# A perceiver block on one core: TensorE's batch loop turned to begin with its products, and the second correction group moved ahead of the seventh key-value part

## The chip, the core and the metric

The kernel runs on one NeuronCore of a Trainium2 chip. That core has TensorE (PE, matrix products), VectorE (DVE), ScalarE (ACT), GpSimd (POOL) and SyncE (SP, which here issues every DMA). Each engine takes its instructions in program order, and they meet only at semaphores. The metric is the device time of one execution in microseconds (us), as the median over runs.

## The reference, cut to what matters

Three residual parts follow each other: a linear cross-attention of 8 × 64 queries on a context of 8 × 1601 rows, a distance attention over the batch, and a mixture of eight experts with causal attention. The change lies in the first part and at its end.

```python
q = (decoder_seq @ Wq.T + bq)          # layer-normed x, 8 batches of 64 rows
k = (encoder_seq @ Wk.T + bk)          # ctx_1024, 8 batches of 1601 rows
v = (encoder_seq @ Wv.T + bv)
kv = jnp.einsum('bthd,bthe->bhde', k, v)            # 16 heads of 32 x 32 per batch
att = jnp.einsum('bqhd,bhde->bqhe', q, kv) * scale
x = x + layer_norm(att + decoder_seq, gamma, beta)
```

## The kernel before, in words

The kernel never forms k and v. For each batch b it makes the Gram matrix G = C^T C of the context (512 x 512), then M = G Wv^T, then the head blocks of Wk M, which are the 16 blocks of kv without bias. Biases come in at the end as "corrections", made from row sums. Every fp32 product of the Gram matrix and of M is split in a high and a low part, so three products stand for one (lines 319 to 321).

On TensorE, one batch is made of these pieces:

- `gram(b)`, lines 844 to 871: 130 products of high and low parts of 13 row groups, about 20 us.
- `products_of(b)`: `m_part(b, 0..3)`, each 12 products of 512 columns (lines 319 to 321), with `mirror(b+1)` (line 885, ten transposes) after the second and `g_transposes(b+1)` (line 892, six transposes) after the fourth.
- `kv_part(b)`, line 923: 64 small fp32 products of 32 columns. The profile has two weight loads and two matmuls for each, so 128 of both, 256 instructions in about 1.3 us. It waits for ACT's copy of the fourth part of M (`m_copy`, line 570).

The pieces of neighbouring batches are interleaved. Batches 0 and 1 are begun in straight code, then a hardware loop (`pe.Fori`, line 951) runs five times over kv_part(b-2), gram(b), products_of(b-1) for b = 2 to 6, and kv_part(5) and gram(7) follow in straight code. In the loop the semaphore counts that are waited for depend on b and are worked out by register instructions. ACT, DVE, POOL and SP have loops of their own and are not turned.

After gram(7) comes the end of the first part, in straight code, written in an order by hand: `row_sums`, m_part(6, 0..3) with `mirror(7)` and `sum_rows` between, `group_corrections(0)` (line 995 two matmuls, line 1001 32 matmuls: batches 0 and 1), `g_transposes(7)`, `kv_part(6)`, `attend(0)` (line 1023), `group_corrections(1)` (batches 2 and 3), m_part(7, 0), `attend(1)`, `group_corrections(2)` (batches 4 to 6), m_part(7, 1), `attend(2)` and so on. group_corrections(n) needs ACT's `right_part(b)` (line 625) for all batches up to the group's last (rb_done), and the kept kv of these batches (kv_done). ACT's `group_spread(1)` (line 643) then spreads the result for `attend(1)`. ACT's order there: three right_parts, m_copy(6, 3), `last_gh_high` (lines 631, 632, 634: the high part of the last Gram matrix), four right_parts, group_spread(1). DVE makes the low part (`last_gl_low`, lines 1516 to 1520, with the copy of kv_part(6) on line 1406 between), which m_part(7, 0) waits for (gl_done). SP loads a weight (`owT`, line 370) once two correction groups are done.

Of the kernel before, what the change touches and what calls it, by code (L numbers as in the profile page):

```python
# [34 lines left out]
def perceiver_block(nc, a, out):  # L35

    B, S, D = a["x"].shape
# [20 lines left out]
    with ExitStack() as ctx:  # L58
# [189 lines left out]
        def head_block(t, c, j):  # L248

            return t[D1 * j:D1 * j + D1, D1 * c:D1 * c + D1]  # L250
# [11 lines left out]
        def right_of(b):  # L262

            return raw[0:64, 4 + b, :] if b < B - 1 else psum_tmp[0:64, :]
# [3 lines left out]
        def group_bank(n):  # L268

            return bank[(1, 2, 4)[n]][:, 0:P * (groups[n][1] - groups[n][0])]  # L270
# [245 lines left out]
        def _(act):  # L516
# [50 lines left out]
            def m_copy(b, ms=range(KC)):  # L567
                for m in ms:
                    act.wait_ge(m_mm, b * 4 + m + 1)
                    act.activation(mb[:, m, :], bank[6 + m % 2][:, :], ACT.Copy).then_inc(m_done, 1)  # L570
# [52 lines left out]
            def right_part(b):  # L623
                act.wait_ge(right_near, 1)
                act.activation(right_of(b), right, ACT.Copy, scale=batch_of[:, b:b + 1]).then_inc(rb_done, 1)

            def last_gh_high():
                act.wait_ge(m_mm, (B - 1) * 4)
                act.wait_ge(gl_done, (B - 1) * 3)
                act.wait_ge(g_add, B * 5)  # L630
                act.activation(upper(ghf, 5 * P), upper(g32f, 5 * P), ACT.Copy).then_inc(gh_done, 1)
                act.activation(last_block(ghf), last_block(g32f), ACT.Copy).then_inc(gh_done, 1)
                act.wait_ge(gt_mm, B)
                act.activation(lower(ghf), mir[:, 0:2, :].rearrange("p m n -> p (m n)")[:, 0:6 * P].rearrange("p (m n) -> p m n", m=3),
                               ACT.Copy).then_inc(gh_done, 1)

            def group_spread(n):

                act.wait_ge(r2_mm, n + 1)
                src = group_bank(n).rearrange("p (m d) -> p m d", d=D1)  # L640
                dst = kv[:, groups[n][0]:groups[n][1], :].rearrange("p b (c j d) -> p (b c) j d", j=4, d=D1)
                for j in range(4):
                    act.activation(dst[:, :, j, :], src, ACT.Copy, scale=headmask[:, D1 * j:D1 * j + 1]).then_inc(r2_act, 1)

            for b in range(3):
                right_part(b)
            m_copy(B - 2, (3,))
            last_gh_high()
            for b in range(3, 7):
                right_part(b)  # L650
            group_spread(1)
            m_copy(B - 1, (0,))
            group_spread(2)
            right_part(B - 1)
# [106 lines left out]
        def _(pe):  # L761
# [112 lines left out]
            def mirror(b):  # L874

                pe.wait_ge(cr_act, b * 2 + 2)
                pe.wait_ge(cr_dve, b + 1)
                c2, c3 = cross[:, 0, :], cross[:, 1, :]
                blk = lambda row, n: row[:, n * P:(n + 1) * P]
                c01 = cross[:, 2, :]  # L880
                for m, row in enumerate(((blk(c01, 0), blk(c01, 2), blk(c2, 0)),
                                         (blk(c01, 3), blk(c2, 1), blk(c3, 1)),
                                         (blk(c2, 2), blk(c3, 2), blk(c01, 1), blk(c3, 3)))):
                    for n, src in enumerate(row):
                        mm = pe.transpose(mir[:, m, n * P:(n + 1) * P], src, ident[:, :])  # L885
                mm.then_inc(mir_mm, 1)

            def g_transposes(b):

                pe.wait_ge(g_add, b * 5 + 5)  # L890
                for n, (row, col) in enumerate(((3, 0), (0, 1), (0, 2), (1, 2), (1, 3), (2, 3))):
                    mm = pe.transpose(mir[:, n // 4, (n % 4) * P:(n % 4 + 1) * P], g32[:, row, col * P:(col + 1) * P], ident[:, :])
                mm.then_inc(gt_mm, 1)

            def m_part(b, m, first):

                if first and m == 0:
                    pe.wait_ge(w_lo, 2)
                    pe.wait_ge(q_done, KC)
                    pe.wait_ge(ld_wk, 16)  # L900
                if m == 0:
                    pe.wait_ge(gl_done, b * 3 + 3)
                if not first and m == 0:
                    pe.wait_ge(kv_done, b)
                if not (first and m < 2):
                    pe.wait_ge(m_done, b * 4 + m - 1)
                for k in range(KC):
                    rows = slice(m * P, (m + 1) * P)
                    mm = three(pe, bank[6 + m % 2][:, :], gh[:, k, rows], gl[:, k, rows], wvh[:, k, :], wvl[:, k, :],
                               k == 0, k == KC - 1)  # L910
                mm.then_inc(m_mm, 1)

            def kv_part(b):

                pe.wait_ge(m_done, b * 4 + 4)
                last = isinstance(b, int) and b == B - 1
                if last:
                    pe.wait_ge(rb_done, B)
                for c in range(KC):
                    for k in range(KC):  # L920
                        for j in range(4):
                            cols = slice(c * P + D1 * j, c * P + D1 * j + D1)
                            mm = pe.matmul(head_block(bank[6], c, j), wk[:, k, cols], mb[:, k, cols],  # L923
                                           start=(k == 0 and not (last and c)), stop=(k == KC - 1 and not last), skip_group_check=last)
                if last:
                    for c in range(KC):
                        for j in range(4):
                            cols = slice(c * P + D1 * j, c * P + D1 * j + D1)
                            mm = pe.matmul(head_block(bank[6], c, j), left[:, cols], right_of(b)[:, cols],
                                           start=False, stop=True, skip_group_check=True)  # L930
                mm.then_inc(kv_mm, 1)

            def products_of(b, first, halfway, between):

                m_part(b, 0, first)
                m_part(b, 1, first)
                halfway()
                m_part(b, 2, first)
                m_part(b, 3, first)
                between()  # L940
# [7 lines left out]
            first_queries((2, 3))  # L948
            gram(1, False)
            products_of(0, True, lambda: mirror(1), lambda: g_transposes(1))  # L950
            with pe.Fori(2, B - 1) as b:
                kv_part(b - 2)
                gram(b, False)
                products_of(b - 1, False, lambda: mirror(b), lambda: g_transposes(b))
            kv_part(B - 3)
            gram(B - 1, False)

            def row_sums():

# [26 lines left out]
            def group_corrections(n):  # L986

                first, end = groups[n]
                if n == 0:
                    pe.wait_ge(bk_near, 1)  # L990
                    pe.wait_ge(rk_near, 1)
                if n == 2:
                    pe.wait_ge(gl_done, 3 * B)
                pe.wait_ge(kv_done, end)
                pe.matmul(group_bank(n), ident[:, :], kv[:, first:end, 0:P], start=True, stop=False, skip_group_check=True)
                pe.wait_ge(rb_done, end)
                at = group_bank(n).rearrange("p (b m) -> p b m", m=P)
                for c in range(KC):
                    for j in range(4):
                        cols = slice(c * P + D1 * j, c * P + D1 * j + D1)  # L1000
                        mm = pe.matmul(at[D1 * j:D1 * j + D1, :, D1 * c:D1 * c + D1], left[:, cols], raw[0:64, 4 + first:4 + end, cols],
                                       start=False, stop=True, skip_group_check=True)
                mm.then_inc(r2_mm, 1)
# [31 lines left out]
            m_part(B - 2, 3, False)  # L1035
            group_corrections(0)
            g_transposes(B - 1)
            kv_part(B - 2)
            attend(0)
            group_corrections(1)  # L1040
            m_part(B - 1, 0, False)
            attend(1)
            group_corrections(2)
# [766 lines left out]
```

## Time and profile before

| | us |
|---|---|
| median of three runs (590.27, 591.0, 598.87) | 591.0 |
| the profiled execution | 589.4 |
| its span | 587.6 |
| TensorE busy | 572.4 (97%) |
| VectorE, ScalarE, GpSimd busy | 346.8, 205.4, 221.2 |

The span runs from the first to the last instruction; 1.8 us of the profiled execution lie around it. The granted TensorE clock is 0.997 of full speed over the whole span, so nothing below hangs on it. "Busy" of TensorE counts matmuls whose ends are modelled. Of the DMA queues, q1 carries the data that SP issues, and q8 and q14 are of the kind "instruction": q8 brings 16 KB at a time (28 packets, 0.46 MB), q14 8 KB.

### The profile page before, as it was taken

To read this page: it belongs to the slowest core of one execution; us is meant where nothing else is said; L and a number is where in the kernel's file an instruction comes from. 1 tells how busy PE (TensorE), PEld (TensorE's weight loads), DVE (VectorE), ACT (ScalarE), POOL (GpSimd) and SP (SyncE) were. 2 spreads that over 40 slices of the span, in tenths; PEclk is the share of its full clock that TensorE was granted. 3 is DMA by queue.
4 is the path that set the end of the run, shared out by engine and by line. 5 is a ranking of instruction groups with operands and counts; after the bars stand their busy time and mean duration, and the time that the engine had idled before them with its cause. 6 is when DMAs were issued, how large, how long until landed. Compare 5 with 4: busy or idle time off the path is not lost.

```text
span 587.6 us, 11551 instructions
## 1 busy us (share of the span) xinstructions
PE 572.4 (97%) x4910; PEld 490.0 (83%) x4910; DVE 346.8 (59%) x405; ACT 205.4 (35%) x294; POOL 221.2 (38%) x182
## 2 busy tenths in 40 slices
PE   6999999999999999899999999999999999999997
PEld 6989888898989889797678987977888887888886
DVE  4896771826546182652687357567777346875741
ACT  4534343505234350522652351423441122434320
POOL 2599963565627265560425000203334543000000
PEclk9999999999999999999999999999999999999999
DMA  8763423142213324004210401206722312898601
GB/s 308 278 239 126 153 86 140 71 152 71 76 76 104 119 71 152 1 1 161 52 72 3 154 3 71 74 1 160 207 72 78 137 72 71 172 260 209 149 0 71
DMA packets 25284, 65.76 MB, mean 112 GB/s; under 512 B 2424, under 2 KB 2424, under 8 KB 22304
## 3 DMA queue, kind: packets, MB, share of 16 engines
q1 hardware_dynamic: 25248, 65.23, 34.9%
q8 instruction: 28, 0.46, 0.4%
q14 instruction: 8, 0.07, 0.1%
HBM read 64.05 MB, written 1.18 MB: 111 GB/s over the span
## 4 chain that ended last, share of the span: by engine, by line
PE 82%; POOL 5%; DVE 4%; issue 1%; POOLq 0%; ACT 0%; DVEq 0%
PE ps L319 17%; PE ps L321 16%; PE ps L320 16%; PE ps L844 8%; POOL psum_tmp L457 4%; PE ps L867 3%; PE ps L871 3%; PE ps L859 2%; PE ps L923 2%; PE ps L854 2%; PE ps L853 2%; PE ps L858 2%; PE ps L1141 1%; PE ps L885 1%; PE ps L1125 1%
## 5 line engine op out<-in xcount | busy, mean ns | idle before, releaser
L457 POOL TENSOR_TENSOR psum_tmp<-psum_tmp,raw 128x512 f32<-128x512 f32 (+1 forms) x88 | 139.7, 1588 | 31.9 <-DVE lo L1364 23.4
L844 PE MATMUL ps<-hi 128*128 128x256 f32 (+3 forms) x416 | 129.5, 313 | 4.9 <-ACT hi L536 4.9
L844 PEld LDWEIGHTS ps<-hi 128*128 128x128 f32 (+1 forms) x416 | 78.7, 190 | 5.3 <-ACT hi L536 4.9
L1364 DVE TENSOR_TENSOR lo<-raw,hi 128x2048 fp32r<-128x2048 f32 (+1 forms) x29 | 61.7, 2158 | 24.4 <-ACT hi L528 24.4
L319 PE MATMUL ps<-hi,gh 128*128 128x512 f32 x192 | 75.7, 394 | 0.0
L321 PE MATMUL ps<-hi,gl 128*128 128x512 f32 x192 | 74.8, 390 | 0.0
L320 PE MATMUL ps<-lo,gh 128*128 128x512 f32 x192 | 74.8, 390 | 0.0
L509 POOL TENSOR_TENSOR sx<-sx,raw 128x512 f32<-128x512 f32 x32 | 41.0, 1288 | 82.4 <-DVE raw L1701 82.4
L731 ACT ACTIVATE hi<-raw 128x2048 fp32r<-128x2048 f32 x14 | 26.8, 1913 | 91.9 <-PE ps L321 91.9
L319 PE MATMUL ps<-wvh,gh 128*128 128x512 f32 x128 | 51.1, 399 | 0.0
L321 PE MATMUL ps<-wvh,gl 128*128 128x512 f32 x128 | 50.1, 391 | 0.0
L320 PE MATMUL ps<-wvl,gh 128*128 128x512 f32 x128 | 50.0, 390 | 0.0
L528 ACT ACTIVATE hi<-raw 128x2048 fp32r<-128x2048 f32 (+1 forms) x29 | 44.0, 1559 | 10.3 <-DMA raw<-in_ctx 10.3
L1707 DVE TENSOR_TENSOR lo<-raw,hi 128x2048 fp32r<-128x2048 f32 x15 | 34.3, 2289 | 19.7 <-ACT hi L731 19.7
L544 ACT ACTIVATE par<-ps 128x512 f32<-128x512 f32 x14 | 7.6, 595 | 101.6 <-PE ps L871 101.6
L319 PEld LDWEIGHTS ps<-hi,gh 128*128 128x128 f32 x192 | 36.0, 188 | 7.8 <-issue 0.2
L321 PEld LDWEIGHTS ps<-hi,gl 128*128 128x128 f32 x192 | 36.0, 188 | 7.5
L320 PEld LDWEIGHTS ps<-lo,gh 128*128 128x128 f32 x192 | 36.1, 188 | 7.3
L867 PE MATMUL ps<-lo,hi 128*128 128x512 f32 (+1 forms) x104 | 41.5, 399 | 0.0
L1370 DVE COPY par<-ps 128x512 f32<-128x512 f32 x8 | 5.5, 690 | 60.7 <-PE ps L871 60.7
L871 PE MATMUL ps<-lo,hi 128*128 128x512 f32 (+1 forms) x104 | 41.2, 396 | 0.0
L439 POOL TENSOR_TENSOR rstd<-vareps,expo 128x1 f32<-128x1 f32 x16 | 11.6, 724 | 78.0 <-DVE vareps L1341 78.0
(228 smaller groups left out, 1204.7 us busy)
## 6 DMA issues: line engine op xcount, KB each, us to landing
raw<-in_ctx SPq DMA_DIRECT2D x23, 1024.0 KB, 4.8
raw<-in_ve SPq DMA_DIRECT2D x8, 1024.0 KB, 5.4
raw<-in_oe SPq DMA_DIRECT2D x8, 1024.0 KB, 5.8
wk<-gm_rows SPq DMA_DIRECT2D x8, 512.0 KB, 9.4
g<-gm_rows SPq DMA_DIRECT2D x8, 512.0 KB, 10.2
raw<-in_ctx SPq DMA_DIRECT2D x8, 130.0 KB
xres<-in_x SPq DMA_DIRECT2D x1, 1024.0 KB, 9.5
mb<-in_WqT SPq DMA_DIRECT2D x1, 1024.0 KB, 13.1
```

The source lines that it names most:

```text
L319: pe.matmul(dst, wh, xh, start=first, stop=False)
L320: pe.matmul(dst, wh, xl, start=False, stop=False)
L321: return pe.matmul(dst, wl, xh, start=False, stop=last)
L457: pool.tensor_tensor(psum_tmp[0:k, :], (raw[:, 0, :] if t == 1 else psum_tmp[0:k, :]), raw[0:k, t, :], ALU.add).then_inc(ctx_sum, 1)
L509: pool.tensor_tensor(v, v, tmp[:, i % 2, :].rearrange("p (h k) -> p h k", k=D2), ALU.add).then_inc(v_added, 1)
L528: act.activation(hi[0:k, r, :], raw[0:k, r, :], ACT.Copy).then_inc(ctx_hi, 1)
L731: act.activation(hi[:, half(w % 2), :], raw[:, half(w % 2), :], ACT.Copy).then_inc(w_hi, 1)
L844: pe.matmul(dst, hi[0:kk, t, cols], x, start=start and opens, stop=stop and closes, skip_group_check=True)
L867: pe.matmul(mir[:, 0, :], w, lb, start=start, stop=stop, skip_group_check=True)
L871: mm = pe.matmul(mir[:, 1, :], w, lb, start=start, stop=stop, skip_group_check=True)
L1364: dve.tensor_tensor(lo[0:k, r, :], raw[0:k, r, :], hi[0:k, r, :].bitcast(F32), ALU.subtract).then_inc(ctx_lo, 1)
L1707: dve.tensor_tensor(lo[:, half(w % 2), :], raw[:, half(w % 2), :], hi[:, half(w % 2), :].bitcast(F32), ALU.subtract).then_inc(w_lo, 1)
```

## The change

The loop on TensorE is turned. kv_part(0) and gram(2) stand ahead of it in straight code, and each of its five passes (b = 3 to 7) runs products_of(b-2), kv_part(b-2), gram(b). The pieces are executed in the order of before; only the place of the loop's back edge moves, from behind the Gram transposes to behind gram. Apart from that, group_corrections(1) moves from behind attend(0) to ahead of kv_part(6), and on ACT one more right_part comes ahead of m_copy(6, 3), and group_spread(1) comes directly behind last_gh_high.

```diff
@@ scalar engine @@
-            for b in range(3):
+            for b in range(4):
                 right_part(b)
             m_copy(B - 2, (3,))
             last_gh_high()
-            for b in range(3, 7):
+            group_spread(1)
+            for b in range(4, 7):
                 right_part(b)
-            group_spread(1)
             m_copy(B - 1, (0,))
             group_spread(2)
@@ tensor engine @@
             products_of(0, True, lambda: mirror(1), lambda: g_transposes(1))
-            with pe.Fori(2, B - 1) as b:
+            kv_part(0)
+            gram(2, False)
+            with pe.Fori(3, B) as b:
+                products_of(b - 2, False, lambda: mirror(b - 1), lambda: g_transposes(b - 1))
                 kv_part(b - 2)
                 gram(b, False)
-                products_of(b - 1, False, lambda: mirror(b), lambda: g_transposes(b))
-            kv_part(B - 3)
-            gram(B - 1, False)
@@
             group_corrections(0)
             g_transposes(B - 1)
+            group_corrections(1)
             kv_part(B - 2)
             attend(0)
-            group_corrections(1)
             m_part(B - 1, 0, False)
```

How the loop's end stands in TensorE's program before (ISA, REGISTER_ALU and the branches are register and branch instructions; every MATMUL row is a product, with its semaphores in brackets): the Gram transposes, the back edge, then kv_part(5) in straight code.

```order
L890 REGISTER_ALU
L892 MATMUL ps<-ident,g 128x128 [waits g_add]
L892 MATMUL ps<-ident,g 128x128 x5
L951 REGISTER_ALU
L951 COMPARE_AND_BRANCH
L923 MATMUL ps<-mb,wk 32x32 [waits m_done]
L923 MATMUL ps<-mb,wk 32x32 x63
```

The same transposes and the kv part behind them in the changed program, where they are inside the loop (gram follows, with its register instructions on line 818 and its counts worked out at run time).

```order
L890 ISA
L892 MATMUL ps<-ident,g 128x128 [waits g_add]
L892 MATMUL ps<-ident,g 128x128 x5
L915 REGISTER_ALU
L923 MATMUL ps<-mb,wk 32x32 [waits m_done]
L923 MATMUL ps<-mb,wk 32x32 x63
L818 ISA
L831 REGISTER_ALU [waits ctx_lo]
```

The straight copy of kv_part and gram has moved from behind the loop to ahead of it, and the first copy of kv_part behind a `products_of` in straight flow of addresses is now in the loop's first pass. Both programs have the same number of TensorE instructions up to row_sums (line 965).

The end of the first part on TensorE, before: the transposes of the last Gram matrix, kv_part(6), attend(0), then the second correction group.

```order
L892 MATMUL ps<-ident,g 128x128 [waits g_add]
L892 MATMUL ps<-ident,g 128x128 x5
L923 MATMUL ps<-mb,wk 32x32 [waits m_done]
L923 MATMUL ps<-mb,wk 32x32 x63
L1023 MATMUL ps<-kv,qT 64x128 [waits r2_dve,g_add,mir_mm]
L1023 MATMUL ps<-kv,qT 64x128 x7
L995 MATMUL ps<-kv,ident 128x256 [waits kv_done]
L1001 MATMUL ps<-raw 32x2x32 [waits rb_done]
L1001 MATMUL ps<-raw 32x2x32 x15
```

The same stretch of TensorE's program, changed.

```order
L892 MATMUL ps<-ident,g 128x128 [waits g_add]
L892 MATMUL ps<-ident,g 128x128 x5
L995 MATMUL ps<-kv,ident 128x256 [waits kv_done]
L1001 MATMUL ps<-raw 32x2x32 [waits rb_done]
L1001 MATMUL ps<-raw 32x2x32 x15
L923 MATMUL ps<-mb,wk 32x32 [waits m_done]
L923 MATMUL ps<-mb,wk 32x32 x63
L1023 MATMUL ps<-kv,qT 64x128 [waits r2_dve,g_add,mir_mm]
L1023 MATMUL ps<-kv,qT 64x128 x7
```

The correction group (17 fp32 products, so 68 instructions) now stands between the transposes and kv_part(6).

## Rows read from the trace of the kernel before

**Rows 1.** The page: the chain that ended last, by engine.
```profile
PE 82%; POOL 5%; DVE 4%; issue 1%; POOLq 0%; ACT 0%; DVEq 0%
```

**Rows 2.** Waits of TensorE: us in total, times, longest ("issue": nothing profiled was waited for).
```profile
PE ps L844 <- ACT hi L536: 4.9, 1, 4.9
PE ps L923 <- issue: 2.8, 2, 1.6
```

**Rows 3.** Timeline at the first back edge: start us, us, engine, line, operation.
```profile
109.38 0.82 PE L892 MATMUL ps<-ident,g 128*128 128x128 f32 x6
109.58 0.60 ACT L570 ACTIVATE mb<-ps 128x512 f32<-128x512 f32 x1 [2.13 <-PE ps L321]
110.22 1.30 PE L923 MATMUL ps<-mb,wk 128*32 128x32 f32 x128
```

**Rows 4.** TensorE's sequencer, lines 951 and 902: ns min/median/max, first and last start.
```profile
L951 PEldq COMPARE_BRANCH  x5: 76/208/239, 109.3 to 245.5; - x5
L902 PEldq FUSED_REGOPS  x5: 51/51/51, 94.6 to 230.8; - x5
```

**Rows 5.** Timeline of TensorE at the product behind gram(2) and at kv_part(0).
```profile
97.34 0.40 PE L319 MATMUL ps<-wvh,gh 128*128 128x512 f32 x1
76.18 1.30 PE L923 MATMUL ps<-mb,wk 128*32 128x32 f32 x128
```

**Rows 6.** Timeline of TensorE at kv_part(5), behind the loop.
```profile
246.48 1.26 PE L923 MATMUL ps<-mb,wk 128*32 128x32 f32 x124
249.39 0.26 PE L923 MATMUL ps<-mb,wk 128*32 128x32 f32 x4 [1.64 <-issue]
```

**Rows 7.** Timeline of TensorE from the first correction group to the seventh m_part.
```profile
288.33 0.65 PE L1001 MATMUL ps<-raw 64*32 64x64 f32 x32
289.71 1.16 PE L923 MATMUL ps<-mb,wk 128*32 128x32 f32 x112
292.04 0.33 PE L923 MATMUL ps<-mb,wk 128*32 128x32 f32 x16 [1.16 <-issue]
292.30 1.09 PE L1023 MATMUL ps<-kv,qT 128*64 128x128 f32 x16
293.32 0.70 PE L995 MATMUL ps<-kv,ident 128*128 128x256 f32 x2
293.95 0.65 PE L1001 MATMUL ps<-raw 64*32 64x64 f32 x32
```

**Rows 8.** The chain in order of time, near line 1141 in the second part.
```profile
343.61 1.99 PE ps L1141 x64
345.60 0.27 issue
```

**Rows 9.** DMA queues, windows 246.7 to 246.8, 293.2 to 293.3, 343.5 to 343.6: packets, MB, share.
```profile
q8 instruction: 1, 0.02, 79.9%
...
q8 instruction: 1, 0.02, 58.3%
...
q8 instruction: 1, 0.02, 59.1%
```

**Rows 10.** DMA queues from 88 to 245 us: packets, MB, share of 16 engines.
```profile
q1 hardware_dynamic: 2390, 15.22, 27.0%
```

**Rows 11.** DMA queues, windows 76.9 to 79.3 and 79.3 to 79.6.
```profile
q1 hardware_dynamic: 121, 0.88, 88.1%
...
q8 instruction: 1, 0.02, 21.7%
```

**Rows 12.** DMA queues from 109.6 to 112.9 us, while a context load lands.
```profile
q1 hardware_dynamic: 128, 1.05, 83.7%
```

**Rows 13.** Timeline of ACT and DVE around the last correction groups.
```profile
286.47 1.95 ACT L625 ACTIVATE raw<-raw,batch_of 64x512 f32<-64x512 f32 x3 [0.60 <-DVE raw L1504]
288.32 0.57 ACT L570 ACTIVATE mb<-ps 128x512 f32<-128x512 f32 x1
290.05 0.79 ACT L634 ACTIVATE gh<-ps 128x768 fp32r<-128x768 f32 x1
...
292.43 0.29 DVE L1406 COPY kv<-ps 128x128 f32<-128x128 f32 x1 [0.62 <-PE ps L923]
292.64 0.95 DVE L1520 TENSOR_TENSOR gl<-ps,gh 128x768 fp32r<-128x768 f32 x1
...
294.67 1.57 ACT L643 ACTIVATE kv<-ps,headmask 128x256 f32<-128x256 f32 x4 [1.38 <-PE ps L1001]
298.70 0.69 DVE L1527 TENSOR_TENSOR xn<-xn,ps 128x512 f32<-128x512 f32 x1 [0.36 <-PE ps L1023]
304.35 0.69 DVE L1527 TENSOR_TENSOR xn<-xn,ps 128x512 f32<-128x512 f32 x1 [0.75 <-PE ps L1023]
```

## The prediction

> **What bounds the kernel now.** I read the page's chain first: TensorE has 82% of it [rows 1], so a change counts by what it does to TensorE's waits. The list of TensorE's waits is short: 4.9 us for a first load, and 2.8 us in two waits of kv_part for "issue", which means that nothing profiled was waited for [rows 2]. The rest of the stretch that is changed runs without a gap. So there is little to win, and the two unnamed waits are the largest thing near the edit. They are the subject of most of what follows.
>
> **What the two waits are.** kv_part(5) runs 124 of its 128 pairs of load and matmul, stops for 1.64 us and runs the last 4 [rows 6]. The same code in the loop runs without a stop, as at 110.22 [rows 3]. kv_part(6) stops after 112 pairs, for 1.16 us [rows 7]. Count the instructions in the built program between these two stops: 8 left in kv_part(5), 261 of gram(7) and its wait, 274 from row_sums on to the last transposes, and 224 in kv_part(6), 767 in all, or three times 256 but for one. In the second part a run of line 1141 stops for 0.27 us exactly between its first and second 64 pairs [rows 8], and by the same count that is seven times 256 instructions further. Queue q8 carries single packets of 16 KB [rows 9], 64 bytes for each of 256 instructions. So I read the stops as page ends: TensorE's program comes in pages of 256 instructions, and the next one was not there yet.
>
> The times fit. A packet of q8 starts in the window 246.7 to 246.8 and work resumes at 249.39, 2.7 us later; the one in 343.5 to 343.6 comes 2.3 us ahead of its resumption at 345.87; after the resumption at 292.04 the next packet starts in 293.2 to 293.3, so 1.2 us lie between entering a page and the start of the packet that brings the following one [rows 7 to 9]. Together a page arrives 3.5 to 3.9 us after the page before it is entered. 256 instructions of kv_part take 1.3 us, of gram some 20 us. Only the former outruns the supply, and a stop depends on where a page ends in the program, and on whether the next page has been there before.
>
> **Part 1, the turned loop.** The order of the pieces stays. The back edge moves. Its branch takes 0.21 us, 0.24 at most [rows 4]. Before, it lay under the Gram transposes and ACT's copy, which ends at 110.18, just ahead of kv_part at 110.22 [rows 3]. After, it lies behind gram. There the sequencer is far ahead: it does the register work of line 902 at 94.6, and TensorE starts the product behind it at 97.34 [rows 4, 5], a lead of 2.7 us. The branch is hidden under that, so I cost it at 0 (0.24 x 4 = 1 us if the cover were gone).
>
> Does the loop stay in memory? Before, a pass has 661 instructions, 2.6 pages, and spans four pages. From 88 to 245 us the only queue at work is q1, with no packet of q8 at all [rows 10], so four pages at least are kept over four back edges. (The Trainium skill, "Runtime: NRT & Kernel Launch", section "Instruction fetch mechanics", says that a taken branch whose target is outside the current two-page window forces a fetch of the target page before execution goes on. This trace disagrees: such branches, 661 instructions back, took 0.24 us at most and fetched nothing. By that rule each back edge, behind gram too, would cost the fetch less the lead; I do not use it.)
>
> Now the pages. The straight copy ahead of the loop is as long as the one that stood behind it, and both programs have the same count up to row_sums, so the page ends stay where they were. Before, kv_part(5) began just behind a page's beginning and reached its end after 248 instructions, in pages never seen. After, kv_part(1), in the loop's first pass, stands in that place, seven instructions earlier, because register instructions now stand in the gram behind it. The page ends 255 instructions into it. The page behind is new in that pass too. So the stop of 1.64 us leaves kv_part(5), which is now a repeat, and comes at the end of kv_part(1), at about 111.4. In passes 2 to 5 it is gone.
>
> The difference is what the DMA engines do. At 246 they were idle. At 110.5, when the packet would start (page entered right behind the transposes, where the sequencer stood at the branch at 109.3 [rows 4], plus 1.2), a load of context has begun: 1.05 MB in 109.6 to 112.9, 83.7% of all 16 engines [rows 12]. What load does to such a packet is seen at kv_part(0): it starts at 76.18, enters a page after some 140 of 256 instructions, at 76.9, and the packet would start at 78.1; but the engines are 88.1% busy until 79.3, and it starts in 79.3 to 79.6 [rows 5, 11], 1.3 us late. Bounds: no delay (0), and until the load is through at 112.9, 2.4 us. I take 1.3, the nearest row: same code, same kind of load. The stop at kv_part(1) becomes 1.64 + 1.3 = 2.9 us. Part 1 costs -1.64 + 2.9 = +1.3 us, between 0 and +2.4.
>
> **Part 2, the moved correction group.** The group is 68 instructions, and took 1.28 us from 293.32 to 294.60 [rows 7]. It goes from behind attend(0) to ahead of kv_part(6), so TensorE's work is unchanged. Its inputs: rb_done of four batches. Three right_parts take 286.47 to 288.42, the fourth ends at 289.07; the transposes end at about 289.7, so nothing waits. ACT's copy for kv_part(6) slips by 0.65 from 288.32 to 288.97 and ends at 289.55 [rows 13], while kv_part(6) now begins at 289.71 + 1.24 = 290.95. The SP load of owT, which waits for this group, is issued some 3.5 us earlier, to idle engines.
>
> The gain is in the stop. The page end now lies 156 instructions into kv_part(6) instead of 224, reached at 290.95 + 78 x 0.0104 = 291.75. The page arrives at 292.04 as before, since it was asked for in group_corrections(0), which stays. The stop shrinks from 1.16 to 0.3 us; kv_part(6) ends 50 pairs later, at 292.55 instead of 292.30, and attend(0) at 293.6. Then m_part(7, 0), which began at 294.60, waits for DVE: the copy after kv_part(6) (292.43, now 292.65) and the low part of line 1520 (0.95 from 292.64, now to 293.8) [rows 13]. It begins at 293.95: -0.65 us.
>
> Does it last? DVE's work for tile 1 waited 0.36 us for attend(1) (at 298.70), and DVE itself is now 0.2 later, so there only 0.15 is won. For tile 2 it waited 0.75 us for attend(2) (304.35) [rows 13], and from there on it is TensorE again that leads, with the whole 0.65. group_spread(1) no longer matters: it began at 294.67 and is 3.3 us earlier now. Part 2: -0.65, between -0.8 (the whole rest of the stop) and 0 (DVE as the leader).
>
> **Sum.** -1.64 + 2.94 - 0.65 = +0.65 us. The span of 587.6 becomes 588.25, the profiled execution's 589.4 becomes 590.05. The median of the runs is 1.6 above that execution, so 591.7.
>
> **The rivals.**
> - The packet is not held up by the load, since a single packet may be served between those of the load. Part 1 is then 0, the sum -0.65: 590.3. Against it stands the row at 79.3. 0.2.
> - The stop disappears: the page behind kv_part(1) is fetched early, for instance if the transition is one instruction off and lies in gram's slower stream, whose first matmuls cover part of it. -1.64 - 0.65 = -2.3: 588.7. For it speaks only that the page end is one instruction from kv_part's end. 0.1.
> - The loop does not fit. The body begins at the end of one page and ends 12 instructions into its fourth, and entering that one asks for a fifth. (Before, the body ended 7 instructions into its fourth page, and nothing was fetched in the passes [rows 10], so that entry may come too close to the branch to ask.) If only four are kept, the fifth displaces the page to which the branch goes back. Each of four back edges then costs 3.9 less the lead of 2.7, 1.2 us, and each later kv_part again a stop of 1.64 to 4.1: 4 x (2.8 to 5.3) = 11 to 21 us, so 603 to 613. Deciding is whether a fifth page fits. For it: the trace shows four kept, not five. 0.06. (The Trainium skill, "Advanced Engine Details and Errata", section "ISA Cache", gives 128 KB on TensorE with 16 KB lines, which is eight pages; it also says "only 2 cache lines", which this trace contradicts.)
> - The correction group, moved, gains nothing: ACT's order (0.65 later to the high part of the last Gram matrix, line 634 ends 291.5) or DVE becomes the leader. +1.3: 592.3. 0.1, close to the forecast.
>
> **How the numbers follow.** Forecast 0.54, the rivals 0.2, 0.1, 0.06 and 0.1. All but the third stand within 3 us of 591, far inside 2% (11.8 us, about what a measurement of this kernel tells from no change). The range: low 589.3, which is 590.3 less 1 for the scatter (the lowest run before is 0.7 under the median) and leaves out most of the vanished stop; high 594.5, which is the loaded bound 591.0 + 2.4 - 0.65 = 592.8 plus 1.7 for scatter. It leaves out 0.06 for the loop and about 0.1 for the vanished stop. Slower by over 2%: 0.05, nearly all of the third rival. Faster: 0.01. Same: 0.94.
>
> **What would show it.** In the changed profile: no wait for issue at 247 to 249; instead one at the end of the kv_part near 110.2, of 1.6 to 4.1 us, with a q8 packet between 110.4 and 113; no q8 packets in the four passes after; no gap between gram and the next product. In kv_part(6) a stop after 78 pairs, near 0.3 us; m_part(7, 0) no later than 0.65 us ahead of its old distance from the last transposes. Packets of q8 in every pass would show the third rival, no stop at all the second. The forecast is wrong if the stops are not page ends.

## The result and the profile after

The changed kernel takes 595.1 us as the median of 18 runs, the kernel before, in the same comparisons, 591.2 us (18 runs). The ratio is 1.0061, with a 95% interval of 1.0043 to 1.0079, so 2.5 to 4.7 us slower: within 2%, but clear of noise, and above the range. The forecast was +0.65 us. The profiled execution took 595.3 us, with a span of 593.6.

The chain that ended last, by engine, of the page after; it answers to [rows 1].

```profile
PE 85%; DVE 6%; POOL 4%; issue 2%; ACT 1%; DMA 1%; POOLq 0%; DVEq 0%
```

TensorE's waits after (us in total, times, longest), which answer to [rows 2]. The waits for "issue" in kv_part have grown to one of 3.6 us and one of 0.2.

```profile
PE ps L923 <- issue: 3.8, 2, 3.6
PE ps L1114 <- issue: 0.4, 1, 0.4
PE ps L319 <- DVE gl L1520: 0.2, 1, 0.2
```

Timeline of TensorE after, kv_part(1) and the first products of gram(3) behind it (start, duration, operation). Before, the same place was gapless [rows 3].

```profile
111.42 1.28 PE L923 MATMUL ps<-mb,wk 128*32 128x32 f32 x127
116.27 0.21 PE L923 MATMUL ps<-mb,wk 128*32 128x32 f32 x1 [3.57 <-issue]
116.49 0.68 PE L844 MATMUL ps<-hi 128*128 128x384 f32 x1
```

The stop comes after 127 of 128 pairs, where the page end was counted to be. The packet for it starts in the window 113.8 to 113.9; from 111.4 to 113.8 only q1, the context load, had packets:

```profile
q8 instruction: 1, 0.02, 61.5%
...
q1 hardware_dynamic: 105, 0.86, 92.0%
```

Then comes what the prediction did not have. Busy time by window after (PE, PEld, DVE, ACT, POOL, granted clock, DMA share, GB/s): at about 116.0, when TensorE had stood still for 3.3 us, the granted clock falls to half, 1.2 instead of 2.4 GHz, and it stays there until 119.4. The first `gram` matmul takes 0.68 us instead of 0.43.

```profile
112.00:116.00 4.00, 0.70 (x83) 0.60 (x72) 2.81 (x3) 4.00 (x5) 1.94 (x2) 0.99 0.57 233
116.00:119.40 3.40, 3.12 (x11) 2.75 (x11) 2.63 (x3) 1.66 (x2) 0.00 (x0) 0.50 0.03 5
119.40:122.00 2.60, 2.60 (x19) 2.50 (x18) 2.60 (x2) 0.00 (x0) 2.57 (x1) 1.00 0.00 0
```

The end of the first part, TensorE and DVE after; it answers to [rows 7, 13].

```profile
295.10 0.88 PE L923 MATMUL ps<-mb,wk 128*32 128x32 f32 x78
296.21 0.64 PE L923 MATMUL ps<-mb,wk 128*32 128x32 f32 x50 [0.22 <-issue]
296.77 1.09 PE L1023 MATMUL ps<-kv,qT 128*64 128x128 f32 x16
297.09 0.95 DVE L1520 TENSOR_TENSOR gl<-ps,gh 128x768 fp32r<-128x768 f32 x1
298.09 0.50 PE L319 MATMUL ps<-wvh,gh 128*128 128x512 f32 x1 [0.23 <-DVE gl L1520]
```

The two timelines laid side by side, at the start of the same work, show where 5.93 us of span went:

| work | before, us | after, us | lag | what lies between |
|---|---|---|---|---|
| kv_part(1) | 110.22 | 111.42 | 1.20 | first gram and transposes, untouched by the change |
| kv_part(2) | 144.28 | 150.61 | 6.33 | +5.13: stop 3.57, the rest (half clock) 1.56 |
| kv_part(5) | 246.48 | 252.73 | 6.25 | -0.08: three rounds of the loop, nothing |
| row_sums | 269.59 | 273.96 | 4.37 | -1.88: kv_part(5) without its stop |
| attend(1) | 297.49 | 301.05 | 3.56 | -0.81: kv_part(6) |
| distances, line 1114 | 331.23 | 334.78 | 3.55 | nothing |
| distances, line 1088 | 340.11 | 345.86 | 5.75 | +2.20: half clock twice as long, stop of 0.42 |
| end of the span | 587.64 | 593.57 | 5.93 | +0.18 |

From the start of kv_part(1) to the start of gram(3) it is 5.07 us instead of 1.24, so by the starts the stop costs 3.83, and half clock behind it 1.30. In the same way 1.86 of the -1.88 us lie between the starts of kv_part(5) and gram(7), though the row of the stop gives 1.64.

The last but one line has its cause in the clock too. Before, the granted clock is half from 335.7 to 339.1, after from 337.8 to 344.7 (windows of both, before first):

```profile
335.70:339.10 3.40, 3.40 (x19) 3.40 (x18) 2.12 (x4) 2.31 (x3) 0.00 (x0) 0.50 0.00 0
```

```profile
337.80:344.70 6.90, 6.90 (x33) 6.90 (x34) 2.48 (x4) 2.97 (x5) 0.00 (x0) 0.51 0.01 2
```

That place and the 1.20 us at the start vary from execution to execution of one kernel (below), so 5.93 us of the profiled pair is more than the 3.6 us of the ratio.

### The profile page after: what moved, and what is told of

It reads as the page before. It is cut to its first block, busy times and chain, and to the rows that moved or that the text cites. A ratio compares the mean times of both kernels' runs of the same rounds, so it can differ in the third digit from the quotient of the medians.

```text
span 593.6 us, 11551 instructions
## 1 busy us (share of the span) xinstructions
PE 576.4 (97%) x4910; PEld 493.8 (83%) x4910; DVE 347.3 (59%) x405; ACT 205.2 (35%) x294; POOL 218.8 (37%) x182
## 4 chain that ended last, share of the span: by engine, by line
PE 85%; DVE 6%; POOL 4%; issue 2%; ACT 1%; DMA 1%; POOLq 0%; DVEq 0%
PE ps L319 16%; PE ps L321 16%; PE ps L320 16%; PE ps L844 9%; POOL psum_tmp L457 4%; PE ps L867 4%; PE ps L871 4%; PE ps L859 2%; PE ps L854 2%; PE ps L853 2%; PE ps L858 2%; PE ps L923 2%; PE ps L885 1%; PE ps L1141 1%; PE ps L1125 1%
## 5 line engine op out<-in xcount | busy, mean ns | idle before, releaser
L457 POOL TENSOR_TENSOR psum_tmp<-psum_tmp,raw 128x512 f32<-128x512 f32 (+1 forms) x88 | 137.9, 1567 | 33.4 <-DVE lo L1364 24.9
L844 PEld LDWEIGHTS ps<-hi 128*128 128x128 f32 (+1 forms) x416 | 79.9, 192 | 9.1 <-ACT hi L536 4.8
```

What stands on the lines that cost most here:

```text
L457: pool.tensor_tensor(psum_tmp[0:k, :], (raw[:, 0, :] if t == 1 else psum_tmp[0:k, :]), raw[0:k, t, :], ALU.add).then_inc(ctx_sum, 1)
L844: pe.matmul(dst, hi[0:kk, t, cols], x, start=start and opens, stop=stop and closes, skip_group_check=True)
```

## The experiments

The theory after the result: the stop at a page end moved from kv_part(5) to kv_part(1), where the page's packet waits for a context load, and the stop is so long that TensorE's clock halves behind it. The rivals: the moved correction group costs; the back edge or the counts worked out at run time cost; the place in a first pass costs in any case.

### One part of the change alone

`e1_turn_only` is the change without its last hunk and without ACT's order, `e2_group_only` the change without the turned loop.

> TensorE's loop turned as in the change, the correction group and ACT's order left as before. Theory PAGE (a stop at a program page's end moved from kv_part(5) to kv_part(1), where a context load holds the page up, and TensorE then runs at half clock for a while): no stop in kv_part(5), one of 3.4 to 3.8 us at the end of kv_part(1), then 3.4 us at half clock (1.6 us lost), and the old stop of about 1.2 us in kv_part(6) smaller or gone, since the page behind gram's end is asked for in the first pass; in all +2.5 to +4 us against before. Rival GROUP (the moved correction group is what costs): no more than +0.5 us. Rival BRANCH (the back edge behind gram and the counts worked out at run time cost): each pass longer than before by the same amount, no single stop.

Measured: 595.4 us (12 runs), ratio 1.0058 (1.0022 to 1.0094). The loss is in the loop. Timeline of TensorE at kv_part(1):

```profile
112.06 1.28 PE L923 MATMUL ps<-mb,wk 128*32 128x32 f32 x127
117.54 0.21 PE L923 MATMUL ps<-mb,wk 128*32 128x32 f32 x1 [4.21 <-issue]
```

The half clock lasted 6.8 us here, from 116.3 to 123.1, and not 3.4. The rounds behind are as long as before (102.18 us from kv_part(2) to kv_part(5), before 102.20). The stop in kv_part(6) did not go, as I had allowed for; it is 0.96 us, presumably since its page is asked for behind gram(7) as before. GROUP and BRANCH fall. Two of the 12 executions, of 587.7 and 589.0 us, lie 6 us or more below the ten others (595.0 to 596.4), with a mean clock of 0.997 where those have 0.991 or 0.994. It looks as if the long stop is missing in some executions; neither of the two was profiled.

> The correction group moved ahead of kv_part(6), with ACT's order, the loop left as before. PAGE: the stop of 1.64 us in kv_part(5) stays, the one in kv_part(6) comes after 78 pairs and is 0.2 to 0.5 us; -0.5 to -0.9 us against before. GROUP: slower than before by 2 us or more, with a wait of TensorE between 289 and 300 us.

Measured: 590.5 us (12 runs), ratio 0.9983 (0.9954 to 1.0011), so a point value of -1.0 us that is not clear of noise. In its profile m_part(7, 0) starts 293.43 - 288.83 = 4.60 us after the end of the first correction group; before it was 5.6 [rows 7]. The group in its new place took 1.11 us. kv_part(6) took 1.60 us instead of 1.30, too little for a stop of its own in the list, so here the remainder is 0.3 us. One thing went against the expectation: kv_part(5) ran all 128 pairs without a stop. The packet had come in an earlier pass, in the window 182.3 to 182.4:

```profile
248.19 1.30 PE L923 MATMUL ps<-mb,wk 128*32 128x32 f32 x128
...
q8 instruction: 1, 0.02, 61.2%
```

So the 1.64 us that the forecast took out of kv_part(5) are not in every execution. One more execution of the kernel before was profiled.

> The kernel before once more (one comment differs), for a second look at one execution. Theory RACE (the page behind the loop is asked for when the sequencer comes within 8 instructions of its taken branch, which in some executions goes through in one of the passes and in others only at the exit): the q8 packet that came at 246.7 us comes in another pass or again at 246.7; where it comes in a pass, kv_part(5) has no stop and the execution is 1.6 us shorter. Rival FIXED: packet and stops stand where they stood, within 0.3 us.

Measured: one execution of 591.8 us, span 590.1. Packet in 247.9 to 248.0, and the stop at the same pair:

```profile
247.63 1.26 PE L923 MATMUL ps<-mb,wk 128*32 128x32 f32 x124
250.28 0.26 PE L923 MATMUL ps<-mb,wk 128*32 128x32 f32 x4 [1.39 <-issue]
```

So FIXED holds for this execution. The run `e9_idle_before_row_sums` below has the same loop too, and its profile has the same stop (124 pairs, then 1.36 us, with the packet in 247.9 to 248.1). Three of four profiled executions with this loop and these page ends have the stop, that of e2 has not, and RACE rests on it alone. How often the stop is missing is open. This execution was 2.5 us longer than the first, and the granted clock was half for 6.8 us from 335.3, as after the change, and 3.4 us in the first.

### Program pages moved by idle instructions

Semaphore instructions whose condition is met long before were put ahead of TensorE's first product, in time in which it waits for data. They shift the page ends, and are meant to change nothing else. (In kernel.py the two added lines shift what stands behind them by two: 1116 and 1143 are lines 1114 and 1141 of the kernels without them.) The edit, with 64 waits (two to an instruction) for 32 instructions, 32 for 16 and 48 for 24:

```diff
+            for _ in range(64):
+                pe.wait_ge(consts, 1)
             gram(0, True)
```

> The changed kernel with 32 semaphore instructions, all met, ahead of the first product on TensorE, in time in which it waits for data. They move all page ends 32 instructions towards the program's start: kv_part(1) no longer begins with its page, and the next page is asked for some 3 us earlier, before the context load. PAGE: no stop in kv_part(1), (5) or (6), no half clock at 116 us; 2 to 3.5 us faster than before, 5 to 7 us faster than the changed kernel. BRANCH: still slower than before by some 3 us, since the loop is still turned. GROUP: the same.

Measured for the changed kernel with 32: 591.6 us (12 runs), ratio to before 1.0007 (0.9974 to 1.0041). The packet came in 106.1 to 106.2, and kv_part(1), (5) and (6) had no stop. Of the 3.6 us lost 3.2 are back, with the loop still turned, so BRANCH falls. The gain over before did not come: stops of 2.7 and 1.0 us have appeared in the distance part. They are from the longest of the 12 executions (599.0 us, mean clock 0.983), the only one profiled.

```profile
PE ps L1116 <- issue: 2.7, 1, 2.7
PE ps L1143 <- issue: 1.0, 1, 1.0
```

> The kernel before with the same 32 semaphore instructions ahead of its first product. PAGE: the stops of 1.64 us in kv_part(5) and of 1.2 us in kv_part(6) go; 2 to 3.5 us faster than before, and level with the changed kernel that has the 32 instructions, within 0.8 us. BRANCH and GROUP: the stops have another cause and stay, no gain; or the changed kernel with the 32 instructions is slower than this by 3 us.

Measured for the kernel before with 32: 590.35 us (12 runs), ratio 1.0005 (0.9976 to 1.0034). No stop in any kv_part, but 0.8, 0.6 and 0.5 us on lines 1116, 320 and 1143. The expected gain of 2 us or more did not come; the equality with the turned kernel held (1.0007 and 1.0005).

> The kernel before with 16 met semaphore instructions ahead of its first product, so all page ends lie 16 instructions earlier. The page that kv_part(5) runs into is then asked for 24 instructions ahead of the branch, in the first pass, and that of kv_part(6) 16 instructions (some 1.8 us) earlier. Theory PAGE: no stop in kv_part(5), one of at most 0.3 us in kv_part(6); the stops of the distance part change by a few tenths; 1 to 2.5 us faster than before. Rival CONSERVED (the stops only move to the next fast stretch, as with 32 instructions): the distance part gets a stop of 0.8 us or more, no gain.

Measured: 590.55 us (12 runs), ratio 1.0016 (0.9985 to 1.0047), no gain. The packet for kv_part(5) came in 106.2 to 106.3 and its stop is gone. kv_part(6) stopped after 104 pairs, 8 pairs earlier as counted, but still for 1.03 us instead of at most 0.3, and line 1143 stopped for 0.7. CONSERVED is nearer the truth.

```profile
289.60 1.10 PE L923 MATMUL ps<-mb,wk 128*32 128x32 f32 x104
291.73 0.40 PE L923 MATMUL ps<-mb,wk 128*32 128x32 f32 x24 [1.03 <-issue]
```

> The changed kernel with the same 16 instructions. PAGE: the page for the end of kv_part(1) is asked for among the products some 2 us earlier, its packet starts by 109.5 us, before the load; stop of at most 0.5 us, no half clock at 116 us, level with the kernel before that has the 16 instructions within 1 us. Rival BRANCH: 3 us slower than that one.

Measured: 594.0 us (12 runs), ratio 1.0063 (1.0027 to 1.0098). This miss taught the most. Timeline of TensorE:

```profile
111.30 1.21 PE L923 MATMUL ps<-mb,wk 128*32 128x32 f32 x119
116.76 0.34 PE L923 MATMUL ps<-mb,wk 128*32 128x32 f32 x9 [4.24 <-issue]
```

The page end moved by 8 pairs, but the packet still came at 114.5. The sequencer's rows (ns, then first and last start) show why: its register instruction ahead of the transposes (line 890) is at 106.4, that behind them (line 915) at 110.3.

```profile
L890 PEldq FUSED_REGOPS  x5: 37/37/42, 106.4 to 248.3; - x5
...
L915 PEldq ALU_OP  x5: 32/32/32, 110.3 to 252.2; - x5
```

Between them are 12 instructions, of which the first waits for DVE's sum (g_add). It looks as if the sequencer does not go past it, so that a page asked for behind it is asked for at 110.3 or later, when the load begins. With 16 instructions the page begins 3 instructions ahead of line 890, and the ask must come a few instructions later. That can be tested with 8 more.

> The changed kernel with 24 met semaphore instructions ahead of its first product; with 16, kv_part(1) still stopped for 4.2 us. Theory ASK (the sequencer stands at the unmet wait of the Gram transposes, g_add, until 110 us, and asks for a page only some 4 to 10 instructions after it entered the page before, so with 16 instructions the ask still fell behind that wait): with 24 the ask lies ahead of that wait, the packet comes at 105 to 108 us, no stop in kv_part(1), no half clock at 116 us, 2.5 to 4.5 us faster than the changed kernel. Rival DISTANCE (the ask simply comes later than was counted): the packet comes at 113 us or later and the stop of 3.5 us or more stays.

Measured for the changed kernel with 24: 588.5 us (12 runs), against 591.9 for before in the same runs; ratio 0.9959 (0.9929 to 0.9989). The packet came in 104.55 to 104.7, and kv_part(1) ran through:

```profile
110.43 1.30 PE L923 MATMUL ps<-mb,wk 128*32 128x32 f32 x128
111.81 0.43 PE L844 MATMUL ps<-hi 128*128 128x384 f32 x1
```

ASK holds, DISTANCE falls. It is the only version that is clearly faster than the kernel before, by 2.4 us (0.7 to 4.2), and by the two ratios to before it is 1.0% or 6 us below the changed kernel, more than the 2.5 to 4.5 us expected. Stops of 0.9 us each on lines 1143 and 1116 remain. Its profiled execution, of 593.8 us of span, is one of the longest, with half clock for 17 us in the distance part. That stretch begins 2.5 us after the end of a stop of only 0.92 us (timeline, and the window of its 16 middle us):

```profile
344.34 2.41 PE L1143 MATMUL ps<-sx,kv 64*64 64x33 f32 x76 [0.92 <-issue]
...
347.00:363.00 16.00, 15.61 (x154) 13.02 (x153) 7.04 (x11) 4.57 (x6) 0.00 (x0) 0.50 0.20 67
```

### The load held back

> The changed kernel, with SP holding the first context load of batches 4 to 7 until kv_part(b-2) is done (the load at 110 us goes out some 1.5 us later; it is first used at 140 us). Theory LOAD (the page for the end of kv_part(1) is late by 2 us because its packet waits behind the load, and TensorE's clock halves for 3.4 us after so long a stop): packet at 1.2 us after the page before is entered, stop of 1.5 to 2.2 us, no half clock at 116 us; 2 to 4 us faster than the changed kernel, between 1 us faster and 0.5 us slower than before. Rival FIRST PASS (a page met first inside a loop's first pass takes that long in any case): stop of 3.6 us and the half clock stay, the time is that of the changed kernel.

```diff
-            with sp.Fori(2, B) as b:
+            for b in (2, 3):
                 for c in range(CH + 1):
                     next_ctx(b, c)
+            with sp.Fori(4, B) as b:
+                sp.wait_ge(kv_mm, b - 2)
+                for c in range(CH + 1):
+                    next_ctx(b, c)
```

Measured: 589.4 us (12 runs), ratio to before 0.9991 (0.9962 to 1.0020), so some 4 us below the changed kernel. The load went out at 113.4, the packet started in 110.6 to 110.7, and the stop shrank from 3.57 to 1.16 us, with a whole clock behind it. Timeline of TensorE (line 927 is line 923, moved by the edit) and the windows behind:

```profile
110.52 1.28 PE L927 MATMUL ps<-mb,wk 128*32 128x32 f32 x127
112.96 0.19 PE L927 MATMUL ps<-mb,wk 128*32 128x32 f32 x1 [1.16 <-issue]
...
112.00:116.00 4.00, 3.01 (x20) 2.70 (x20) 3.71 (x5) 4.00 (x4) 1.10 (x1) 1.00 0.39 98
116.00:122.00 6.00, 6.00 (x41) 5.69 (x40) 4.81 (x3) 0.77 (x2) 4.89 (x2) 1.00 0.36 126
```

This is the same program of TensorE, with the same page met for the first time in the same pass. FIRST PASS falls; what makes the stop long is the load.

### Half clock without a page

> The kernel before with 125 met semaphore instructions between gram(7) and row_sums, so that TensorE's sequencer is busy for some 6.4 us while TensorE has 2.7 us of work left: TensorE idles 3 to 4 us at 269 us, with no page or load involved in it (the page ends behind it move). Theory CLOCK (so long a stop, whatever its cause, is followed by half clock): the granted clock falls to half within 1 us of the stop's end and stays there for 3.4 us, 1.3 to 1.7 us lost beside the stop. Rival PAGE ONLY (the half clock at 116 us had to do with the late page or the load): clock whole there.

Measured: one execution of 602.7 us. The idle time came out too long: the 125 instructions started some 107 ns apart, and TensorE idled 10.8 us instead of 3 to 4. The granted clock fell to half 2.7 us into the idle time, which began at 270.6, and was back after 287:

```profile
270.60:273.30 2.70, 0.00 (x0) 0.00 (x0) 0.69 (x1) 1.08 (x2) 0.00 (x0) 1.00 1.02 347
273.30:286.90 13.60, 5.54 (x21) 2.27 (x22) 0.02 (x1) 1.79 (x3) 0.00 (x0) 0.50 0.01 3
287.00:300.00 13.00, 13.00 (x66) 8.54 (x65) 7.36 (x10) 3.45 (x5) 1.93 (x2) 1.00 0.27 62
```

The one packet of q8 near it came in 269 to 270, before the idle time. So idle time brings half clock with no late page in it, and PAGE ONLY falls. A context load was under way in its first 2.7 us (the DMA share of 1.02), so the run does not exclude the load; but the loads of the kernel before, as that of [rows 12], had a whole clock behind them. Nor does the run say how a stop of just 3.6 us acts by itself. For that stand the stops in kv_part: those of 3.57, 4.21 and 4.24 us all had half clock at their end, those of 0.2 to 1.6 us none. In the distance part it is not so simple: every profiled execution has a stretch of half clock there, that of the kernel before with no stop ahead of it, and in the profiles of e3 and e10 a second, longer one begins some 2.5 us after stops of 1.04 and 0.92 us. What brings it on there is open.

## Why the prediction was wrong, point by point

- **What the waits are** (page ends): right. All stops of kv_part came at the counted pair (127, 78, 104, 119), and moved with the idle instructions by half their number in pairs.
- **The back edge, cost 0**: right. The three rounds from kv_part(2) to kv_part(5) are 0.08 us apart from before in all, and e3 and e4 are level.
- **The loop stays in memory**: right. From 136 to 293 us q8 has no packet after the change.
- **The stop at kv_part(1), 2.9 us**: the place was right, the size not. The step that failed is the delay of 1.3 us by the load, taken from one row [rows 11]. The packet started 2.4 us after kv_part's start, against 0.1 with the load held back: 2.3 us of delay, near the bound of 2.4. The row at 79.3 was a load near its end; this one met a load at its beginning, and started when 0.13 of some 1.05 MB were left. The stop was 3.57 us instead of 2.9 (4.21 and 4.24 in e1 and e7).
- **The sum**: it has no term for the clock. Of what could be measured, this is the step that cost most: the stop brought 3.4 us of half clock, 1.3 to 1.6 us (6.8 us of it in e1). "Time and profile before" took the mean granted clock of 0.997 as a sign that nothing hung on it; it is a mean over a span, and hid a stretch of half clock in the kernel before already, from 335.7 to 339.1.
- **-1.64 us at kv_part(5)**: the profile had -1.88, but e2 shows an execution of the same loop where there is no such stop to remove, so the average is somewhat less.
- **Part 2, -0.65 us**: right in mechanism and nearly in size, -0.81, with the stop after 78 pairs, 0.22 us, and a wait for DVE's line 1520 as foreseen. The sum gave the group 1.28 us in one place and 1.24 in another; in its new place it took 1.10, from 294.00 to 295.10. In the times this part is not clear of noise: e2 has -1.0 us with 0 inside the interval.
- **By the same steps with measured terms**: 3.57 + 1.56 - 1.88 - 0.81 = +2.4 us, just under the 2.5 to 4.7 of the ratio, whose middle is 3.6. What makes up the difference was not settled. One part may be that the stop in kv_part(5) is missing in some executions of before, as in that of e2, so that less than 1.88 us is taken away on average. The distance part adds little on average, though it differs by 1.7 us in the profiled pair: 15 of 18 executions of the changed kernel have a mean clock of 0.991 (three stretches of 3.4 us in the profiled one, one of them at kv_part(1) and two in the distance part), while of 35 of before 16 have 0.994 (two in the distance part, as in e8) and 10 have 0.997 (one). Over the fast executions that is 3.1 stretches against 1.9, so 0.2 more beside the one at kv_part(1), some 0.3 us: an estimate from the mean clocks.
- **The rivals**: none of them came true. The packet was held up, the stop did not vanish, no page was fetched in passes 2 to 5, and the moved group's part of the profile won 0.81 us.

## What to carry to other kernels

Where an engine runs through hundreds of short instructions, count its program in pages: a stop that shows as "issue" stands at fixed distances in the program, and any edit upstream can move it under a load or away from it. Put such a page's request ahead of long work and of unmet waits, or keep bulk loads away from it. Shifting the pages can also just move a stop: with 16 and 32 idle instructions nothing was gained over before. A long stop (3.6 us and more in kv_part) had a second price behind it, half clock; a sum of waits needs a term for this, and a mean clock near 1 does not exclude it.

## What the runs showed of the hardware that was not expected

- A packet of program that met a 1 MB load started 2.4 us after kv_part(1) did, and the same packet with the load held back 0.1 us after it. (The Trainium skill, "Runtime: NRT & Kernel Launch", section "Instruction fetch mechanics", says that the cost of crossing a block boundary is mostly hidden; here, where kv_part stopped at one, it was 0.2 to 4.2 us.)
- TensorE's sequencer, usually 2.7 us ahead, took 3.9 us from line 890 to line 915, over twelve instructions the first of which waited on a semaphore. That the request for a page behind that point comes only then fits the packet at 114.5 in e7 and at 104.6 in e10; the request itself is in no trace.
- Removing one page stop mostly brought another: with 32 idle instructions in the changed kernel the kv stops went and stops of 2.7 and 1.0 us came on lines 1116 and 1143 (in its longest execution). 16 and 32 gained nothing over before, and 24 gained 2.4 us.
- The packet with the page behind the loop's exit (by the count, the page before it begins 8 instructions ahead of kv_part(5)) came in one of the passes, at 182.3 us, in one profiled execution of four, and at the exit, at 246.7 to 248.1, in the other three.
